# Token halves interleaved in the tail of a fused attention and feed-forward kernel

## The chip, the cores and the metric

The kernel runs on one core of a Trainium2 chip. The metric is the device time of one execution in microseconds (us). The core's engines work from queues of their own and meet only at semaphores: TensorE (PE in the profile), VectorE (DVE), ScalarE (ACT), GpSimd (POOL) and SyncE (SP), which issues all the transfers.

## The reference

The input is x of shape (4, 256, 256), that is 1024 tokens of width 256, and a context of (4, 256, 64). Four blocks follow one another, each with a residual. What matters for the change:

```
x = x + L0_xattn(layernorm(x), ctx, ...)      # 16 heads
x = x + L0_ffn(layernorm(x), w_fc, w_proj)    # both products on values rounded to fp8:
    h = square(relu(fp8(x) @ fp8(w_fc).T));  out = fp8(h) @ fp8(w_proj).T
    # one scale over the whole of h: no token of h can be rounded before all are there
x = x + L1_xattn(ctx, ctx, mask, qc_score=layernorm(x)):
    softmax(mask(((q @ Wq.T + bq) @ (k @ Wk.T + bk).T / 8) * layernorm(x)))
x = x + L1_ffn(layernorm(x)):
    h  = x + (rmsnorm(x) @ wv + bv) @ wo
    h2 = rmsnorm(h)
    y  = h + (silu(h2 @ w_gate) * (h2 @ w_up)) @ w_down    # 704 inner columns
    x where the router's score of the token is not over 0.5
```

After h has been rounded, everything is row by row: token t needs only its own row.

## The kernel before, in words

The 1024 tokens are 8 tiles of 128 (NT = 8). The program is one queue of instructions for each engine, written out by hand; there is no scheduler, and an instruction waits behind every earlier one of its engine. The first attention block fills the first 260 us. The change is in what comes after.

**GpSimd after the attention loop.** It makes the attention mask `mbias` (four steps of two instructions, L460 and L461, one step for each batch), scales the weights `wg` by the second norm's weights (L467), and then raises the variances to the power -1/2 (`power(3)`, L391). On this VectorE's `newton(3)` and the input scale of the feed-forward block wait; GpSimd then makes `xn` from `xs` tile by tile (L475), which ScalarE and VectorE turn into fp8 values `x8`. After that it scales `wu`, and serves eight more powers, in the order of their number. TensorE's `expand` (L1298) makes h from `x8`; VectorE's relu (L871) and ScalarE's square follow.

**Rounding of h.** When the largest of h is known (L890), ScalarE writes two scaled copies of each token tile (L633, L635) and VectorE makes of them the rounded tile `h8` in two instructions over 1024 elements (L978 and L981). TensorE contracts the tile with `wpr8` (L1352, into bank 4 + t % 4), and VectorE adds the product to `xs` and takes its statistics (`x2_tile`, L896 and L899). VectorE's order before is tile by tile: h8(t), then x2_tile(t-2). All eight h8 come first, then the scores of the first half.

**The halves.** From there on the tokens go in two halves of 4 tiles each, `gr` 0 and 1, each through this chain on VectorE, with GpSimd's power and ScalarE between:
- `gate_scores` (L908), `newton`, `mask_scores` (L916), `largest` (L922); ScalarE's exponentials `softmax` (L640)
- `x3_tiles` (L928 to L934) and statistics; `norm_tiles` (newton, L698, L944 to L946)
- TensorE turns `xn` (`turn_norm`, L1055), ScalarE copies it (`turned_copy`, L498), TensorE multiplies with `wvo` (`attend`, L1365)
- `h_tiles` (newton, L955, L957), ScalarE's squares (L651), `h_square` (L962), `h2_tiles` (newton, L971)
- TensorE turns `h2`, ScalarE copies it to `tailT`, and the gate stage begins.

**Gate stage.** 12 steps n = 0 to 11, six for each half: 8 matmuls of 512 columns (L1389), Silu on ScalarE (L662), the product on VectorE (L1016). Step n needs the product of step n-2. The second half's chain hangs between these steps: in all three queues there are lines `if n == 1`, `if n == 2` and so on that say after which step a piece of it comes. VectorE also computes the router's scores (L1027) at n = 4 and adds the base rows (L1036), which GpSimd has summed in one long instruction (L489). Then 8 contractions with `wd` (L1407), each followed by two VectorE instructions and a transfer out.

**Fillers.** `keep_busy(n, spare)` (L1273) issues n matmuls of 512 columns, whose results nobody reads, in TensorE's queue. Before, 6 of them stand ahead of each contraction, 50 after the last x2 and 18 ahead of the turning of h2.

Of the kernel before, what the change touches and what calls it, by code (L numbers as in the profile page):

```python
# [12 lines left out]
ALU = mybir.AluOpType  # L13
# [9 lines left out]
P = 128  # L23
B, S, D = 4, 256, 256
TOK = B * S
NT = TOK // P
# [79 lines left out]
def build(nc, x, ctx_t, ctx_n, blob, const_a, const_b, wq1_t, wk1_t, attn_mask, key_mask,  # L106
          w_fc_t, w_proj_t, small, w_router, wv_t, wo, w_gate, w_up, w_down, out):
    with ExitStack() as ctx:
# [126 lines left out]
        ident16_ready = sem("ident16_ready")  # L235
        norm_ready = sem("norm_ready")
        turned = sem("turned")
# [143 lines left out]
        def _(pool):  # L381
# [67 lines left out]
            for k in range(DK):  # L449
# [6 lines left out]
                                        ALU.mult))  # L456
            for b in range(B):
                mb = mbias[:, 2 * b:2 * b + 2, :]
                kb = ktmp[:, b * S:(b + 1) * S].unsqueeze(1).to_broadcast([P, 2, S])
                in_order(pool.tensor_scalar(mb, mA[:], MASKED, None, ALU.mult))  # L460
                ins = pool.tensor_tensor(mb, mb, kb, ALU.add)  # L461
            ins.then_inc(mbias_ready, 1)


# [4 lines left out]

            pool.wait_ge(d_ffn1, 64)  # L470
            scale_rows(wg)
            power(3, c_ve[:], minus_half[:], c_y[:])
            pool.wait_ge(inv_ready, 1)
            for t in range(NT):
                pool.tensor_scalar(xn[:, t, :], xs[:, t, :], negmean[:, t:t + 1], xscale[:, t:t + 1],  # L475
                                   ALU.add, ALU.mult).then_inc(v_ready, 1)
            scale_rows(wu)

# [4 lines left out]

            for n, gr in ((4, 0), (5, 1), (6, 0), (7, 0), (8, 0), (9, 1), (10, 1), (11, 1)):
                powers(n, gr)

            pool.wait_ge(norm_ready, 3 * NT)
            pool.wait_ge(h2_ready, NT)
# [4 lines left out]
        def _(act):  # L493
# [163 lines left out]
            for n in range(2 * FT1):  # L657
                m = min(P, FF1 - n % FT1 * P)
                act.wait_ge(gate_ready, n + 1)
                if n >= 2:  # L660
                    act.wait_ge(act_ready, n - 1)
                act.activation(silu(n)[0:m, :], bank[2 * (n % 2)][0:m, :], ACT.Silu).then_inc(silu_ready, 1)  # L662
                if n == 1:
                    turned_copy(8, tailT, turned_copied, (2, 3))
                if n == 2:
                    h_squares(1)
                if n == 4:
                    turned_copy(10, tailT, turned_copied, (2, 3))
# [3 lines left out]
        def _(dve):  # L672
# [220 lines left out]
            def x2_tile(t):  # L893

                dve.wait_ge(mlp_ready, t + 1)
                dve.scalar_tensor_tensor(out=xs[:, t, :], in0=bank[4 + t % 4][:, 0:D], scalar=sc[:, 2:3],  # L896
                                         in1=xs[:, t, :], op0=ALU.mult, op1=ALU.add).then_inc(x2_ready, 1)
                dve.wait_ge(x2_ready, t + 1)
                return dve.bn_stats(stats[:, t, :], xs[:, t, :])  # L899
# [5 lines left out]
            def gate_scores(gr):  # L905

                for t in range(*groups[gr]):
                    dve.scalar_tensor_tensor(out=xn[:, t, :], in0=xs[:, t, :], scalar=mv[:, t, 0:1], in1=qk1[:, t, :],  # L908
                                             op0=ALU.subtract, op1=ALU.mult).then_inc(norm_ready, 1)

            def mask_scores(gr):
                lo, hi = groups[gr]
                newton(4 + gr, rstd, lo, hi)
                dve.wait_ge(norm_ready, NT + hi)
# [9 lines left out]
            def x3_tiles(gr):  # L924
# [10 lines left out]
                in_order(ins)  # L935
                aggregate(6 + 3 * gr, lo, hi)

            def norm_tiles(gr):

                lo, hi = groups[gr]  # L940
                newton(6 + 3 * gr, rstd, lo, hi)
                for t in range(lo, hi):
                    normalise(t).then_inc(norm_ready, 1)
                in_order(dve.tensor_tensor(c_ve[:, lo:hi], rstd[:, lo:hi], rstd[:, lo:hi], ALU.mult))  # L944
                in_order(dve.tensor_tensor(c_ve[:, lo:hi], c_ve[:, lo:hi], mv[:, lo:hi, 1], ALU.mult))
                dve.tensor_scalar(c_ve[:, lo:hi], c_ve[:, lo:hi], 1e-6, None, ALU.add).then_inc(variance_ready, 1)  # L946

            def h_tiles(gr):

                newton(7 + 3 * gr, r1, *groups[gr])  # L950
                dve.wait_ge(vo_copied, 3)
                dve.wait_ge(norm_ready, 2 * NT + groups[gr][1])
                for t in range(*groups[gr]):
# [11 lines left out]
            def h2_tiles(gr):  # L965

                lo, hi = groups[gr]
                dve.wait_ge(variance_ready, 8 + 3 * gr)
                newton(8 + 3 * gr, r2, lo, hi)
                for t in range(lo, hi):  # L970
# [3 lines left out]

            for t in range(NT + 2):
                if t < NT:
                    dve.wait_ge(square_ready, t + 1)
                    dve.scalar_tensor_tensor(out=hv[t % 3], in0=hm[t % 3], scalar=1.5 * 2.0 ** 14, in1=hv[t % 3],  # L978
                                             op0=ALU.max, op1=ALU.subtract).then_inc(step_ready, 1)
                    dve.wait_ge(step_ready, t + 1)  # L980
                    dve.scalar_tensor_tensor(out=h8[:, :, t * P:(t + 1) * P],  # L981
                                             in0=hm[t % 3].rearrange("p (f s) -> p f s", f=FT0), scalar=1.5 * 2.0 ** 14,
                                             in1=hv[t % 3].rearrange("p (f s) -> p f s", f=FT0),
                                             op0=ALU.max, op1=ALU.subtract).then_inc(h8_ready, 1)
                if t == NT:

                    dve.wait_ge(mbias_ready, 1)
                    dve.wait_ge(qk_copied, 8)
                    gate_scores(0)
                    mask_scores(0)  # L990
                    largest(0)
                if t >= 2:
                    ins = x2_tile(t - 2)
                if t == half + 1:
                    in_order(ins)
                    aggregate(4, 0, half)
            in_order(ins)
            aggregate(5, half, NT)
# [12 lines left out]

            for n in range(2 * FT1):
# [34 lines left out]
        def _(pe):  # L1047
# [296 lines left out]
            keep_busy(10, 3)  # L1344
            for t in range(NT):
                if t:
                    keep_busy(6, 3)
                pe.wait_ge(h8_ready, t + 1)
                if t >= 4:
                    pe.wait_ge(x2_ready, t - 3)  # L1350
                for ft in range(FT0):
                    ins = pe.matmul(bank[4 + t % 4][:, 0:D], h8[:, ft, t * P:(t + 1) * P], wpr8[:, ft, :],  # L1352
                                    start=(ft == 0), stop=(ft == FT0 - 1))
                ins.then_inc(mlp_ready, 1)


            def turn_norm(c):
                turn(1, lambda t: xn[:, t, :], norm_ready, 2 * NT, (2 * c, 2 * c + 1))

# [20 lines left out]
            for n in range(2 * FT1):  # L1380
# [111 lines left out]
```

## Time and profile before

| | us |
|---|---|
| median of 3 runs | 459.43 (459.09 to 460.18) |
| the profiled execution's own time | 459.85 |
| its span | 458.1 |
| busy: PE / DVE / ACT / POOL | 410.2 / 304.5 / 202.8 / 178.5 |
| chain that ended last, by engine | PE 61%, DVE 20%, ACT 7%, POOL 5% |

The span is what the engines' records cover; the time of the execution is 1.75 us longer. The busy share of PE counts the fillers. In the page's 40 slices (11.45 us each) TensorE is busy 9 tenths or more up to 275 us, with few exceptions; the slices from 275 us on have the digits 5, 6, 9, 6, 8, 6, 3, 9, 8, and 9 after that. The granted clock (PEclk, 9 is full) has 5, 9, 8, 8, 9, 6, 8, 9, 7 in the slices from 286 us on, and 9 after that.

### The profile page before, as it was taken

Reading aid. Unit: us, or ns where it says so; the run is one execution under the profiler, and the core shown is the slowest. Engines: PE = TensorE matmul, PEld = TensorE weight load, DVE = VectorE, ACT = ScalarE, POOL = GpSimd, SP = SyncE. Lnnn points to the kernel's source line nnn. Section 1 sums busy time; section 2 is a strip of 40 time slices with the busy share of each in tenths; the row PEclk is TensorE's granted clock in tenths of the full one; section 3 lists DMA queues with packets and bytes.
Section 4 is the critical chain, followed back from the end, with each engine's and each line's share of the span. In section 5 each row is a group of like instructions: output and inputs, shape, how many; then the busy total and the mean of one; then the engine's idle time right before and its main releaser. Section 6 shows DMA issues by size and latency. Waiting matters only on the chain.

```text
span 458.1 us, 5998 instructions
## 1 busy us (share of the span) xinstructions
PE 410.2 (90%) x2029; PEld 247.9 (54%) x2029; DVE 304.5 (66%) x681; ACT 202.8 (44%) x551; POOL 178.5 (39%) x164
## 2 busy tenths in 40 slices
PE   1898999999999999999999995696863989999997
PEld 1765666666566666665667872342431444634475
DVE  5778679677686766767775653586999576483322
ACT  1525466464565555555578523267931024321100
POOL 2554554655546455464631189630010101040000
PEclk9999999999999999999999999598896897999999
DMA  8643020110201000021000140000000000000011
GB/s 263 213 154 123 2 92 1 49 46 0 93 0 71 24 1 1 0 73 55 1 1 1 26 140 0 0 1 1 0 1 0 0 2 0 0 0 1 1 46 46
DMA packets 9085, 17.51 MB, mean 38 GB/s; under 512 B 2144, under 2 KB 6944, under 8 KB 8160
## 3 DMA queue, kind: packets, MB, share of 16 engines
q1 hardware_dynamic: 9056, 17.14, 11.1%
q8 instruction: 16, 0.26, 0.2%
q14 instruction: 13, 0.11, 0.1%
HBM read 16.09 MB, written 1.05 MB: 37 GB/s over the span
## 4 chain that ended last, share of the span: by engine, by line
PE 61%; DVE 20%; ACT 7%; POOL 5%; issue 4%; DMA 2%; SPq 0%; DVEq 0%; ACTq 0%
PE bank L1389 8%; PE bank L1153 5%; PE bank L1407 5%; PE bank L1178 5%; PE bank L1060 5%; PE bank L1166 4%; PE bank L1062 4%; PE bank L1061 4%; PE bank L1184 4%; DVE rot_up L737 3%; PE bank L1138 3%; PE bank L1273 3%; PE bank L1083 3%; ACT prob L557 3%; DVE tail_all L981 2%
## 5 line engine op out<-in xcount | busy, mean ns | idle before, releaser
L410 POOL TENSOR_TENSOR prob<-prob,rinv 128x512 f32<-128x512 f32 x64 | 66.6, 1042 | 106.4 <-DVE rinv L795 106.4
L557 ACT ACTIVATE prob<-bank,negmax 128x256 f32<-128x256 f32 x128 | 60.1, 480 | 40.6 <-DVE negmax L790 40.6
L790 DVE TENSOR_REDUCE negmax<-bank 128x2 f32<-128x512 f32 x64 | 41.2, 687 | 25.1 <-PE bank L1153 24.6
L391 POOL TENSOR_TENSOR c_y<-c_ve,minus_half 128x4 f32<-128x4 f32 (+1 forms) x11 | 12.8, 1166 | 98.2 <-DVE c_ve L694 69.3
L1389 PE MATMUL bank<-tailT,blobs 128*128 128x512 f32 (+1 forms) x96 | 45.6, 630 | 1.5 <-ACT tailT L498 0.8
L548 ACT COPY probT<-bank 128x512 f32<-128x512 f32 x64 | 37.8, 591 | 19.6 <-PE bank L1166 19.4
L1273 PE MATMUL bank<-wfc,ident 128*128 128x512 bf16 x144 | 40.4, 434 | 6.6 <-DVE xs L896 6.2
L405 POOL TENSOR_TENSOR rot_low<-rot_low,rot_up 128x512 f32<-128x512 f32 x32 | 40.9, 1277 | 12.0 <-DVE rot_up L737 12.0
L737 DVE TENSOR_TENSOR rot_up<-bank,cb 64x512 f32<-64x512 f32 x64 | 44.1, 689 | 0.9
L1060 PE MATMUL bank<-xnT,w 128*128 128x512 f32 x96 | 42.0, 437 | 1.5 <-DVE xnT L713 1.0
L1166 PEld LDWEIGHTS bank<-ca,prob 128*128 128x128 f32 x256 | 30.5, 141 | 18.9 <-issue 16.2
L1166 PE MATMUL bank<-ca,prob 128*128 128x128 f32 x256 | 38.9, 275 | 1.8 <-ACT probT L548 1.1
L735 DVE TENSOR_TENSOR rot_low<-bank,cb 128x512 f32<-128x512 f32 x32 | 22.1, 689 | 26.4 <-PE bank L1062 26.4
L1062 PE MATMUL bank<-xnT,w 128*128 128x512 f32 x96 | 37.9, 395 | 0.0
L1061 PE MATMUL bank<-xnT,w 128*128 128x512 f32 x96 | 37.6, 392 | 0.0
L1178 PE MATMUL bank<-probT,kva 128*64 128x256 f32 x256 | 34.7, 392 | 2.2 <-ACT probT L548 1.4
L1153 PE MATMUL bank<-ktmp,uT 64*128 64x256 f32 x256 | 36.3, 402 | 0.0
L569 ACT COPY cT<-bank 128x256 f32<-128x256 f32 x32 | 11.9, 373 | 46.7 <-PE bank L1178 46.7
L1389 PEld LDWEIGHTS bank<-tailT,blobs 128*128 128x128 f32 (+1 forms) x96 | 18.0, 193 | 26.5 <-issue 24.7
L1184 PE MATMUL bank<-wkvo,cT 128*128 128x256 f32 x128 | 30.9, 384 | 0.5 <-ACT cT L569 0.5
L1153 PEld LDWEIGHTS bank<-ktmp,uT 64*128 64x128 f32 x256 | 22.0, 186 | 13.7 <-issue 12.3
L1273 PEld LDWEIGHTS bank<-wfc,ident 128*128 128x128 bf16 x144 | 15.2, 109 | 24.9 <-issue 8.7
(186 smaller groups left out, 706.7 us busy)
## 6 DMA issues: line engine op xcount, KB each, us to landing
blobs<-in_blob SPq DMA_DIRECT2D x7, 1024.0 KB, 4.8
xs<-in_x SPq DMA_DIRECT2D x2, 512.0 KB, 4.0
xn<-in_w_fc_t SPq DMA_DIRECT2D x1, 1024.0 KB, 4.9
ctxT<-in_w_proj_t SPq DMA_DIRECT2D x1, 1024.0 KB, 5.3
out<-qk SPq DMA_DIRECT2D x8, 128.0 KB, 1.7
cb<-in_const_b SPq DMA_DIRECT2D x1, 768.0 KB, 8.4
blobs<-in_w_gate SPq DMA_DIRECT2D x1, 704.0 KB, 4.2
blobs<-in_w_up SPq DMA_DIRECT2D x1, 704.0 KB, 7.0
```

What stands on the lines that cost most here:

```text
L410: pool.tensor_tensor(p[:], p[:], rinv[:, n % PROBS, :].unsqueeze(2).to_broadcast([P, 2, S]), ALU.mult).then_inc(normed, 1)
L557: ins = act.activation(prob[n % PROBS][:, st, :], pS[n % 2][:, st * S:(st + 1) * S], ACT.Exp, bias=negmax[:, n % 2, st:st + 1], accum_out= ...
L737: ins = dve.tensor_tensor(tokens(crossed[to:to + DC, :]), tokens(src[lo:lo + DC, :]), angles(sinq, r, lo, lo + DC), ALU.mult)
L1060: pe.matmul(o, a[0], b[0], start=start, stop=False)
L1061: pe.matmul(o, a[0], b[1], start=False, stop=False)
L1062: return pe.matmul(o, a[1], b[0], start=False, stop=stop)
L1153: ins = pe.matmul(pS[h][:, st * S:(st + 1) * S], uT[b // 2][lo:hi, at:at + P], ktmp[lo:hi, b * S:(b + 1) * S], start=True, stop=True)
L1166: ins = pe.transpose(pT[:, lt * S + st * P:lt * S + (st + 1) * P], prob[n % PROBS][:, st, lt * P:(lt + 1) * P], ident)
L1178: ins = pe.matmul(pV[b % 2][h * DC:(h + 1) * DC, 0:S], kva[:, 2 * b + lt, :], probT[h][:, lt, :], start=(lt == 0), stop=(lt == 1))
L1184: return pe.matmul(bank[OUT_BANK[t // 2]][:, t % 2 * D:(t % 2 + 1) * D], cT[:, f, t * P:(t + 1) * P], wkvo[:, f, :], start=(f == 0 and t % ...
L1273: pe.matmul(bank[spare][:], ident16[:], wfc8[:, 0, 0:CH], start=True, stop=True)
L1389: ins = pe.matmul(bk[0:m, :], w[:, k, ft * P:ft * P + m], tailT[:, k, c * CH:(c + 1) * CH], start=(k == 0), stop=(k == DK - 1))
```

## The change

The computation is the same. In GpSimd's queue two of the four mask steps and both scalings of weights come after the making of `xn`; the powers are asked for in another order (the first half's four, then the second half's). VectorE's order is written out: the first half's scores come after h8(4) and its own four x2 tiles, and the second half's h8 and x2 tiles stand between the steps of the first half's chain. TensorE's contractions are spread accordingly, with other numbers of fillers, into banks 6 and 7 in place of four banks, which adds a wait for an older x2 tile. In the gate stage the second half's pieces hang on later steps, the router's scores come at n = 6, and the base rows are added two at a time from n = 8.

```diff
 # GpSimd
-            for b in range(B):
+            def mask_rows(b):
...
-            pool.wait_ge(d_ffn1, 64)
-            scale_rows(wg)
+            for b in range(2):
+                mask_rows(b)
             power(3, c_ve[:], minus_half[:], c_y[:])
             pool.wait_ge(inv_ready, 1)
             for t in range(NT):
                 pool.tensor_scalar(xn[:, t, :], ...).then_inc(v_ready, 1)
+            for b in range(2, B):
+                ins = mask_rows(b)
+            ins.then_inc(mbias_ready, 1)
+            pool.wait_ge(d_ffn1, 64)
+            scale_rows(wg)
             scale_rows(wu)
-            for n, gr in ((4, 0), (5, 1), (6, 0), (7, 0), (8, 0), (9, 1), (10, 1), (11, 1)):
+            for n, gr in ((4, 0), (5, 0), (6, 0), (7, 0), (8, 1), (9, 1), (10, 1), (11, 1)):
                 powers(n, gr)
 # ScalarE, in the gate stage
-                if n == 1:
+                if n == 3:
                     turned_copy(8, tailT, turned_copied, (2, 3))
-                if n == 2:
+                if n == 4:
                     h_squares(1)
-                if n == 4:
+                if n == 5:
                     turned_copy(10, tailT, turned_copied, (2, 3))
 # VectorE (x2_tile reads bank[6 + t % 2] in place of bank[4 + t % 4])
-            for t in range(NT + 2):
...
-            x3_tiles(0)
-            gate_scores(1)
-            norm_tiles(0)
-            h_tiles(0)
-            h_square(0)
-            mask_scores(1)
-            h2_tiles(0)
-            largest(1)
-            x3_tiles(1)
-            norm_tiles(1)
+            for t in range(3):
+                h8_tile(t)
+            x2_tile(0)
+            h8_tile(3)
+            x2_tile(1)
+            h8_tile(4)
+            x2_tile(2)
+            in_order(x2_tile(3))
+            aggregate(4, 0, half)
+            dve.wait_ge(mbias_ready, 1)
+            dve.wait_ge(qk_copied, 8)
+            gate_scores(0)
+            mask_scores(0)
+            largest(0)
+            h8_tile(5)
+            x2_tile(4)
+            x3_tiles(0)
+            h8_tile(6)
+            x2_tile(5)
+            norm_tiles(0)
+            h8_tile(7)
+            x2_tile(6)
+            h_tiles(0)
+            h_square(0)
+            in_order(x2_tile(7))
+            aggregate(8, half, NT)
+            h2_tiles(0)
+            gate_scores(1)
+            mask_scores(1)
+            largest(1)
 # VectorE, in the gate stage
-                if n == 2:
+                if n == 0:
+                    x3_tiles(1)
+                if n == 1:
+                    norm_tiles(1)
+                if n == 4:
                     h_tiles(1)
-                if n == 3:
                     h_square(1)
                     h2_tiles(1)
-                if n == 4:
+                if n == 6:
... # the router's scores
-                t = n - 4
-                if 0 <= t:
+                if n >= 8:
                     dve.wait_ge(base_ready, 1)
-                    dve.tensor_tensor(atbuf(t), atbuf(t), qk1[:, t, :], ALU.add).then_inc(base_added, 1)
+                    for t in (2 * n - 16, 2 * n - 15):
+                        dve.tensor_tensor(atbuf(t), atbuf(t), qk1[:, t, :], ALU.add).then_inc(base_added, 1)
 # TensorE
-            for t in range(NT):
-                if t:
-                    keep_busy(6, 3)
+            def contract(t):
                 pe.wait_ge(h8_ready, t + 1)
-                if t >= 4:
-                    pe.wait_ge(x2_ready, t - 3)
+                if t >= 2:
+                    pe.wait_ge(x2_ready, t - 1)
...
-            pe.wait_ge(x2_ready, NT)
-            keep_busy(50, 3)
+            contract(0)
+            for t in range(1, 5):
+                keep_busy(6, 3)
+                contract(t)
+            keep_busy(32, 3)
+            contract(5)
+            keep_busy(16, 3)
+            contract(6)
+            keep_busy(4, 3)
             turn_norm(0)
             attend(0)
-
+            contract(7)
             pe.wait_ge(wgu_ready, 2)
-            keep_busy(18, 7)
+            keep_busy(14, 4)
             turn(2, hbuf, h2_ready, 0, (0, 1))
...
-                if n == 1:
+                if n == 3:
+                    pe.wait_ge(x2_ready, NT)
                     turn_norm(1)
-                if n == 2:
+                if n == 4:
                     attend(1)
-                if n == 4:
+                if n == 5:
                     turn(2, hbuf, h2_ready, 0, (2, 3))
```

Left out are the new numbers of the semaphore counts, which follow the new order, and a semaphore `gate_done` that counts the products of L908, which `norm_ready` counted before.

## Rows read from the trace of the kernel before

**Rows 1.** Chain that ended last, 255 to 300 us: start us, length us, what.
```profile
282.10 4.05 POOL blobs L467 x2
286.16 1.64 POOL c_y L391
290.81 1.93 PE bank L1318 x4
```
**Rows 2.** Timeline, 255 to 296 us: start us, length us, engine and line [idle before].
```profile
279.78 0.17 DVE L694 TENSOR_SCALAR c_ve<-mv 128x8 f32<-128x8 f32 x1
287.89 0.17 DVE L684 TENSOR_TENSOR c_t<-c_y 128x8 f32<-128x8 f32 x1 [7.39 <-POOL c_y L391]
```
**Rows 3.** Timeline of VectorE, rounding of h to the first half's scores.
```profile
297.95 0.88 DVE L865 SCALAR_TENSOR_TENSOR tail_all<-bf_m,xn 128x256 bf16<-128x256 bf16 x1
...
334.33 0.48 DVE L896 SCALAR_TENSOR_TENSOR xs<-bank,sc,xs 128x256 f32<-128x256 f32 x1
...
337.57 0.48 DVE L896 SCALAR_TENSOR_TENSOR xs<-bank,sc,xs 128x256 f32<-128x256 f32 x1
...
345.67 1.66 DVE L908 SCALAR_TENSOR_TENSOR xn<-xs,mv,qk 128x256 f32<-128x256 f32 x4
...
349.73 1.22 DVE L922 TENSOR_REDUCE c_m<-xn 128x4 f32<-128x1024 f32 x1
```
**Rows 4.** Timeline of VectorE, the first half's chain after its exponentials.
```profile
353.30 0.18 DVE L928 RECIPROCAL c_r<-ssq 128x4 f32<-128x4 f32 x1
...
356.96 0.17 DVE L694 TENSOR_SCALAR c_ve<-mv 128x4 f32<-128x4 f32 x1
...
359.57 1.38 DVE L698 TENSOR_SCALAR xn<-xs,mv,rstd 128x256 f32<-128x256 f32 x4
...
361.25 0.17 DVE L946 TENSOR_SCALAR c_ve<-c_ve 128x4 f32<-128x4 f32 x1
...
368.75 0.48 DVE L955 SCALAR_TENSOR_TENSOR cT<-bank,r,cb 128x256 f32<-128x256 f32 x1 [5.44 <-PE bank L1365]
...
372.83 0.17 DVE L962 TENSOR_SCALAR c_ve<-ssq 128x4 f32<-128x4 f32 x1 [0.57 <-ACT mbias L651]
...
375.43 0.16 DVE L684 TENSOR_TENSOR c_t<-c_y 128x4 f32<-128x4 f32 x1
...
376.22 1.14 DVE L971 TENSOR_SCALAR cT<-cT,r 128x256 f32<-128x256 f32 x4
```
**Rows 5.** Timeline of TensorE, 290 to 460 us.
```profile
352.25 13.63 PE L1273 MATMUL bank<-wfc,ident 128*128 128x512 bf16 x50 [6.25 <-DVE xs L896]
...
367.48 3.72 PE L1365 MATMUL bank<-cb,tailT 128*128 128x256 f32 x16 [0.73 <-ACT tailT L498]
...
379.00 10.08 PE L1389 MATMUL bank<-tailT,blobs 128*128 128x512 f32 x16 [0.82 <-ACT tailT L498]
...
405.58 7.28 PE L1389 MATMUL bank<-tailT,blobs 128*64 128x512 f32 x16
413.58 17.58 PE L1389 MATMUL bank<-tailT,blobs 128*128 128x512 f32 x40 [0.72 <-DVE cT L1016]
431.08 1.99 PE L1407 MATMUL bank<-wd,tail_all 128*128 128x256 f32 x8
```
**Rows 6.** Timeline of ScalarE, between the second exponentials and the first Silu.
```profile
380.84 1.28 ACT L662 ACT_TABLE_LOAD   x1
```
**Rows 7.** Busy time by stretch: PE, PEld, DVE, ACT, POOL; PEclk is the granted clock.
```profile
375.00:379.00 4.00, 1.63 (x9) 0.97 (x9) 3.32 (x10) 1.22 (x3) 0.00 (x0) 0.89 0.01 2
379.00:382.00 3.00, 3.00 (x4) 1.45 (x5) 1.11 (x4) 2.98 (x9) 0.00 (x0) 0.50 0.00 0
```
**Rows 8.** Timeline of VectorE at the router's first score.
```profile
405.35 4.43 DVE L1027 SCALAR_TENSOR_TENSOR ctxT<-xn,wr 128x256 f32<-128x256 f32 x1
```
**Rows 9.** Timeline of GpSimd, 270 to 460 us.
```profile
339.22 2.07 POOL L391 TENSOR_TENSOR c_y<-c_ve,minus_half 128x4 f32<-128x4 f32 x1 [37.35 <-DVE c_ve L694]
...
404.98 4.51 POOL L489 TENSOR_TENSOR qk<-xs,xn 128x2048 f32<-128x2048 f32 x1 [2.18 <-DVE cT L971]
```

More of the change, by code:

```diff
@@ L235, in build @@
         ident16_ready = sem("ident16_ready")
-        norm_ready = sem("norm_ready")
+        norm_ready, gate_done = sem("norm_ready"), sem("gate_done")
         turned = sem("turned")
@@ L460, in _ @@
                 in_order(pool.tensor_scalar(mb, mA[:], MASKED, None, ALU.mult))
-                ins = pool.tensor_tensor(mb, mb, kb, ALU.add)
-            ins.then_inc(mbias_ready, 1)
+                return pool.tensor_tensor(mb, mb, kb, ALU.add)
             def scale_rows(w):
@@ L482, in powers @@
                 power(n, c_ve[:, lo:hi], minus_half[:, lo:hi], c_y[:, lo:hi])
-            for n, gr in ((4, 0), (5, 1), (6, 0), (7, 0), (8, 0), (9, 1), (10, 1), (11, 1)):
+            for n, gr in ((4, 0), (5, 0), (6, 0), (7, 0), (8, 1), (9, 1), (10, 1), (11, 1)):
                 powers(n, gr)
-            pool.wait_ge(norm_ready, 3 * NT)
+            pool.wait_ge(norm_ready, 2 * NT)
             pool.wait_ge(h2_ready, NT)
@@ L895, in x2_tile @@
                 dve.wait_ge(mlp_ready, t + 1)
-                dve.scalar_tensor_tensor(out=xs[:, t, :], in0=bank[4 + t % 4][:, 0:D], scalar=sc[:, 2:3],
+                dve.scalar_tensor_tensor(out=xs[:, t, :], in0=bank[6 + t % 2][:, 0:D], scalar=sc[:, 2:3],
                                          in1=xs[:, t, :], op0=ALU.mult, op1=ALU.add).then_inc(x2_ready, 1)
@@ L908, in gate_scores @@
                     dve.scalar_tensor_tensor(out=xn[:, t, :], in0=xs[:, t, :], scalar=mv[:, t, 0:1], in1=qk1[:, t, :],
-                                             op0=ALU.subtract, op1=ALU.mult).then_inc(norm_ready, 1)
+                                             op0=ALU.subtract, op1=ALU.mult).then_inc(gate_done, 1)
             def mask_scores(gr):
                 lo, hi = groups[gr]
-                newton(4 + gr, rstd, lo, hi)
-                dve.wait_ge(norm_ready, NT + hi)
+                newton(4 + 4 * gr, rstd, lo, hi)
+                dve.wait_ge(gate_done, hi)
                 for t in range(lo, hi):
@@ L935, in x3_tiles @@
                 in_order(ins)
-                aggregate(6 + 3 * gr, lo, hi)
+                aggregate(5 + 4 * gr, lo, hi)
             def norm_tiles(gr):
                 lo, hi = groups[gr]
-                newton(6 + 3 * gr, rstd, lo, hi)
+                newton(5 + 4 * gr, rstd, lo, hi)
                 for t in range(lo, hi):
@@ L948, in h_tiles @@
             def h_tiles(gr):
-                newton(7 + 3 * gr, r1, *groups[gr])
+                newton(6 + 4 * gr, r1, *groups[gr])
                 dve.wait_ge(vo_copied, 3)
-                dve.wait_ge(norm_ready, 2 * NT + groups[gr][1])
+                dve.wait_ge(norm_ready, NT + groups[gr][1])
                 for t in range(*groups[gr]):
@@ L967, in h2_tiles @@
                 lo, hi = groups[gr]
-                dve.wait_ge(variance_ready, 8 + 3 * gr)
-                newton(8 + 3 * gr, r2, lo, hi)
+                dve.wait_ge(variance_ready, 7 + 4 * gr)
+                newton(7 + 4 * gr, r2, lo, hi)
                 for t in range(lo, hi):
                     dve.tensor_scalar(hbuf(t), hbuf(t), r2[:, t:t + 1], None, ALU.mult).then_inc(h2_ready, 1)
-            for t in range(NT + 2):
[L976 to L996, printed above, removed]
@@ L997, in _, with h8_tile @@
-            in_order(ins)
-            aggregate(5, half, NT)
+            def h8_tile(t):
+                dve.wait_ge(square_ready, t + 1)
+                dve.scalar_tensor_tensor(out=hv[t % 3], in0=hm[t % 3], scalar=1.5 * 2.0 ** 14, in1=hv[t % 3],
+                                         op0=ALU.max, op1=ALU.subtract).then_inc(step_ready, 1)
+                dve.wait_ge(step_ready, t + 1)
+                dve.scalar_tensor_tensor(out=h8[:, :, t * P:(t + 1) * P],
+                                         in0=hm[t % 3].rearrange("p (f s) -> p f s", f=FT0), scalar=1.5 * 2.0 ** 14,
+                                         in1=hv[t % 3].rearrange("p (f s) -> p f s", f=FT0),
+                                         op0=ALU.max, op1=ALU.subtract).then_inc(h8_ready, 1)
@@ L1344, in _ @@
             keep_busy(10, 3)
-            for t in range(NT):
-                if t:
-                    keep_busy(6, 3)
+            def contract(t):
                 pe.wait_ge(h8_ready, t + 1)
-                if t >= 4:
-                    pe.wait_ge(x2_ready, t - 3)
+                if t >= 2:
+                    pe.wait_ge(x2_ready, t - 1)
                 for ft in range(FT0):
-                    ins = pe.matmul(bank[4 + t % 4][:, 0:D], h8[:, ft, t * P:(t + 1) * P], wpr8[:, ft, :],
+                    ins = pe.matmul(bank[6 + t % 2][:, 0:D], h8[:, ft, t * P:(t + 1) * P], wpr8[:, ft, :],
                                     start=(ft == 0), stop=(ft == FT0 - 1))
@@ L1357, in turn_norm @@
             def turn_norm(c):
-                turn(1, lambda t: xn[:, t, :], norm_ready, 2 * NT, (2 * c, 2 * c + 1))
+                turn(1, lambda t: xn[:, t, :], norm_ready, NT, (2 * c, 2 * c + 1))
             def attend(c):
```

## Prediction

> **What bounds the kernel now.** I read the page's slices first. TensorE is busy nearly everywhere up to 275 us, and not in the slices behind it: whatever the change gains, it gains there. Then the chain that ended last, for who sets the time in those slices, and then each engine's timeline, for durations. Two places stand out.
>
> First, after the attention loop the chain runs through GpSimd. The variances are written at 279.78 + 0.17 = 279.95 [rows 2], but GpSimd is still at mask steps and at scaling `wg` (until 286.15), and only then raises them to the power, 1.64 us [rows 1]. VectorE sits idle 7.39 us ahead of 287.89 [rows 2]. The next steps (maximum over partitions, input scale, `xn`) hang on that one value.
>
> Second, from 320 to 352 us VectorE is the bound: it rounds a tile of h and adds a tile of x2 every 337.57 - 334.33 = 3.24 us [rows 3], while ScalarE and GpSimd have nothing to do and TensorE mostly runs fillers. Then it turns round: 50 fillers start at 352.25, when the last x2 is there, and take 13.63 us [rows 5]; `xn` of the first half is ready at 359.57 + 1.38 = 360.95 [rows 4], and TensorE reaches it only at about 365.9. VectorE idles 5.44 us ahead of 368.75 [rows 4]. From 379.00 on TensorE is nearly solid: 52.08 us to the start of the down projections at 431.08 [rows 5], and those last to the end.
>
> **The change part by part.** I work on the clock of the trace of before, in which VectorE reaches x2_tile(2) at 334.33, and take GpSimd's part off at the end.
>
> *GpSimd's order.* Two mask steps (as before) end ahead of 279.95, so power(3) starts about there and not at 286.16 [rows 1]: 6.1 us earlier, and VectorE's newton with it, since its other operands were there when the 7.39 us of idle time began. What is late next? TensorE's four matmuls of L1318 took 1.93 us [rows 1] after a long idle stretch; with the pause 6 us shorter I expect full clock there, half the time, and ScalarE, which waited for them, gains up to 0.7 us against GpSimd's tiles. Against it stands what GpSimd now does beside the rounding of x8: two mask steps and two scalings that are no longer behind it or ahead. VectorE's L863 and L865 read two tensors in SBUF. Beside GpSimd's two-input instruction such an instruction waited until that ended: 4.43 us in place of some 0.4 beside L489 [rows 8, 9]. Beside GpSimd's one-input scaling two of eight were lengthened, to 0.88 as in [rows 3]. So the two L461 instructions can each hold VectorE up for their length, of which I count about 0.7 in all. Bounds: 0 and 2.5. The two small terms cancel: 6.1 us. The rest of GpSimd's work ends some 9 us later than its old place and lies beside relu (which reads PSUM and SBUF once) and before the first user of `mbias`; it hides. Its wait for the weights' transfers costs nothing, as they landed before 282; SyncE's queue isn't touched.
>
> The Trainium skill (SBUF — State Buffer, Who interferes with whom) says that a VectorE instruction with two SBUF inputs and a GpSimd instruction that reads SBUF exclude each other for the whole of the one that came first. The row of L1027 agrees; the eight instructions beside the scaling, most of them at their usual length, do not bear it out in full.
>
> *First half's scores earlier.* x2_tile(2) starts at 334.33 as before. h8(5) no longer stands between: x2_tile(3) ends at 336.05, statistics and aggregate to 336.75, the scores block runs 345.67 to 350.95 = 5.28 [rows 3], so `largest` ends at 342.0; if the power runs as long as its longest (2.07 against 1.0 [rows 9]) 0.5 later. I take 342.15. Exponentials take the 2.1 us to 344.25, behind h8(5) on VectorE (3.24 - 0.86 = 2.38 [rows 3]), which ends at 344.5. The x2 of tile 4 to 345.35. x3_tiles: 353.30 to 357.13 = 3.83 [rows 4], to 349.25. h8(6) and x2(5) 3.24, to 352.5; they cover the power, even at 2.07. norm_tiles: newton 0.79 (375.43 to 376.22), then 359.57 to 361.42 = 1.85 [rows 4], to 355.1. h8(7) and x2(6) to 358.35, newton to 359.15.
>
> TensorE meanwhile: xn's fourth tile at 354.6, turning and copies some 1.5 (for h2 it was 377.36 to 379.00 = 1.64 [rows 4, 5]), so attend starts at 356.05 and takes 3.72 [rows 5] to 359.8. h_tiles is bound by VectorE: 368.75 to 372.26 is 3.5 [rows 4], so 359.15 to 362.6; h_square 0.57 later [rows 4], 363.45. The power of 1.0 and newton of 0.8 cover x2(7) and the aggregate (1.5). h2 starts at 365.8, against 376.22 [rows 4]: 10.4 us earlier. The new waits of contract(t) for x2(t-2) cost 0.4 us or less in TensorE's queue, where nothing but fillers is behind. The fillers: 32 take 7.2 us at full clock (50 took 13.63 with the first 5 us at half clock [rows 5]) against the 8.6 us until h8(5); 16 take 3.6 against 6.1. So contractions come on time, with pauses of 1.4 and 2.5 us. Those can bring the clock down ahead of attend(0): at half clock all through, attend ends at 363.5, h_tiles 2.0 us later than said. Range 0 to 2.0; nearest is 0, as VectorE has 1.9 us of slack on attend's last tile.
>
> *Gate stage.* It starts 10.4 us earlier, at 368.6 for 379.00 [rows 5]. VectorE does the second half's scores after h2 (367.0 + 5.3 = 372.3), exponentials to 374.4, table load 1.28 [rows 6], first Silu ready 376.4, product 377.1. The first matmul group took 6.6 us of the 10.08 [rows 5] at half clock [rows 7], so to 375.2: no stall from the new order. x3_tiles(1) 3.83 delays the second product to 381.6; step 3 needs it at 382.1. norm_tiles(1) ends 384.8, turning 386.4, attend(1) is after step 4: 389.8 to 393.3. Silu and product of step 4, newton, h_tiles, squares, power, newton: h2 of the second half at 398.1. Step 5 (3.4 us) ends on TensorE at 396.8: 1.4 us of stall. Turning and copies 2.8 (376.22 to 379.00 [rows 4, 5]), which no matmul step covers now: step 6 starts at 400.8. Before it started at 409.2 (half of the 7.28 us from 405.58 [rows 5]). So of 10.4 us 2.0 are given back: 8.4. The 0.72 us ahead of 413.58 [rows 5] goes, since the product of step 5 no longer waits behind a router score that GpSimd's L489 holds up [rows 8, 9]; the scores now come at step 6 (some 2.9 us), when L489 (from 399.2 on, 4.51) is done. 9.1. Steps 7 to 11 and the down projections are TensorE-bound as before; two base additions per step (0.7 us) fit in 3.4.
>
> *The clock.* From 396.8 to 400.8 TensorE has a pause, thin transposes and a pause. That is the pattern of 375 to 379 us, 1.63 us busy of 4.00, after which the clock was 0.50 [rows 7] for some 6.4 us, which cost 3.2. The other such place before, around 404 us, had no drop, but its pause was only 0.4. Ends 0 and 3.2; the rows allow either, the likeness is to the first, the phase is open. I take half, 1.6.
>
> Sum: 6.1 + 9.1 - 1.6 = 13.6. On the profiled execution (459.85, span 458.1) that is 446.2; it stands 0.4 above the median, so on the median 459.43 I say 445.8.
>
> **The rivals.**
>
> *A, the exclusive lock holds for every pair.* Then each of the seven or so roundings of x8 left when the masks resume waits for a whole GpSimd instruction: 2 x 1.5, 2 x 1.3, 3 x 2.0 (L467 is 4.05 for two [rows 1]) = 11.6 in place of 3.0, 8.6 lost: 454.4. For: the 4.43 [rows 8]. Against: only two of eight lengthened beside the scaling. It is what the page cited above would give.
>
> *B, GpSimd's head start is lost* because another input of the scale chain is late (TensorE's vo products or a table on ScalarE): 3 us of 6.1 remain, 448.9. Against: VectorE's 7.39 idle us name only the power.
>
> *C, the clock never recovers between 336 and 384* (slower). Fillers are counts, so at half clock 32 take 13.7 us and 16 take 6.8: contract(6) at 359, turning at 363, attend to 373, contract(7) and 14 fillers to 381, step 0 at 384 instead of 379.00. With the longer gate stage (53.4 for 52.1 us) and its drop of 3.2 the down projections start 9.5 us later, less 6.1: 3.4 slower, 462.8. It decides from the point at which the 32 fillers outlast h8(5) by more than 7 us. Against it: in the page's slice at 332 us TensorE is busy 6 tenths, with the same 3.24 us cycle, and its clock has the full digit.
>
> *D, the second half's chain is longer than worked out*: every us by which h2(1) is late is a us of TensorE's stall. If two of its hand-offs cost 1.5 us more each, and the clock drops fully: 450.5.
>
> **How the numbers follow.** Forecast with its clock cases 0.70 (442.5 to 449.0), A 0.08, B 0.07, D 0.10, C 0.03, and 0.02 that the parts cancel to nothing. 442 to 451 leaves out A, C and the rest, with something for misses on the fast side: about 2 in 10. A change within 0.2% is what a measurement can't tell from none. Faster 0.95, same 0.01, slower 0.04.
>
> **What would show it.** GpSimd's eight-column power starts within 0.3 us of the variances. The first half's exponentials come some 15 us earlier than before (8.8 here and 6.1 by GpSimd). 32 fillers end before h8(5). Step 0 of the gates 16.5 us earlier than 379.00, step 6 about 14.5 earlier than 409.2 with TensorE idle ahead of it. The clock after step 6's start says which end of the 3.2 us it is. Wrong would be: VectorE's L863 and L865 near 1.3 us each, contractions waiting on fillers, or a stall ahead of step 3.

## The result, and the profile after

The changed kernel takes 445.38 us in the median of four runs (443.75 to 446.39), against 459.26 (458.03 to 460.18): a ratio of 0.970, 95% interval 0.9676 to 0.9724, or 13.9 us less. The prediction was 445.8. The profiled execution is the fastest of the four, 443.75 with a span of 442.0, so its trace shows 16.1 us of span, not 13.9. Here and below, executions over 1.5% slower than the fastest of the same kernel are left out of the ratios, not out of the medians.

The trace of after, along the path. First GpSimd and VectorE around the power of the variances (timeline; start, length, engine, line, what ended the idle time before):

```profile
279.06 0.17 DVE L697 TENSOR_SCALAR c_ve<-mv 128x8 f32<-128x8 f32 x1
279.31 1.67 POOL L391 TENSOR_TENSOR c_y<-c_ve,minus_half 128x8 f32<-128x8 f32 x1 [3.55 <-DVE c_ve L697]
281.08 0.17 DVE L687 TENSOR_TENSOR c_t<-c_y 128x8 f32<-128x8 f32 x1 [1.27 <-POOL c_y L391]
285.45 0.44 DVE L866 SCALAR_TENSOR_TENSOR xn<-bf_m,xn 128x256 f32<-128x256 bf16 x1 [1.15 <-ACT bf_m L588]
291.27 0.82 DVE L866 SCALAR_TENSOR_TENSOR xn<-bf_m,xn 128x256 f32<-128x256 bf16 x1
292.92 1.41 DVE L868 SCALAR_TENSOR_TENSOR tail_all<-bf_m,xn 128x256 bf16<-128x256 bf16 x1
295.14 0.69 DVE L874 TENSOR_SCALAR_CACHE_REDUCE cT<-bank 128x512 f32<-128x512 f32 x1 [0.81 <-PE bank L1309]
```

GpSimd now waits for the variances (3.55 us), not they for it, and the 7.39 us of VectorE's idle time in [rows 2] are 1.27. The two long roundings (0.82 and 1.41 us) are the price beside the mask steps.

VectorE in the interleaved stretch:

```profile
326.84 0.48 DVE L899 SCALAR_TENSOR_TENSOR xs<-bank,sc,xs 128x256 f32<-128x256 f32 x1
333.36 1.22 DVE L925 TENSOR_REDUCE c_m<-xn 128x4 f32<-128x1024 f32 x1
337.74 0.16 DVE L931 RECIPROCAL c_r<-ssq 128x4 f32<-128x4 f32 x1
351.41 0.48 DVE L958 SCALAR_TENSOR_TENSOR cT<-bank,r,cb 128x256 f32<-128x256 f32 x1
357.96 1.14 DVE L974 TENSOR_SCALAR cT<-cT,r 128x256 f32<-128x256 f32 x4
368.36 0.69 DVE L1024 TENSOR_TENSOR tail_all<-bank,tail_all 128x512 f32<-128x512 f32 x1 [4.05 <-ACT tail_all L665]
```

L958 has no idle time before it any more (5.44 in [rows 4]): from 326.84 to 357.96 VectorE is the bound, with its longest wait 0.57 us, ahead of L965.

TensorE, fillers (L1284) and gate stage (L1404):

```profile
328.33 7.07 PE L1284 MATMUL bank<-wfc,ident 128*128 128x512 bf16 x32
344.12 1.68 PE L1361 MATMUL bank<-wpr,tail_all 128*128 128x256 bf16 x8 [2.59 <-DVE tail_all L984]
360.74 7.10 PE L1404 MATMUL bank<-tailT,blobs 128*128 128x512 f32 x16 [0.82 <-ACT tailT L501]
369.11 3.70 PE L1404 MATMUL bank<-tailT,blobs 128*128 128x512 f32 x8 [1.26 <-DVE tail_all L1024]
373.56 3.70 PE L1404 MATMUL bank<-tailT,blobs 128*128 128x512 f32 x8 [0.75 <-DVE tail_all L1024]
390.27 1.55 PE L1066 MATMUL bank<-ca,cT 128*128 128x128 f32 x8 [1.68 <-DVE cT L974]
392.56 22.49 PE L1404 MATMUL bank<-tailT,blobs 128*128 128x512 f32 x48 [0.73 <-ACT tailT L501]
414.98 1.99 PE L1423 MATMUL bank<-wd,tail_all 128*128 128x256 f32 x8
```

Busy time by stretch, with the granted clock as the third number from the end of the line:

```profile
345.00:347.00 2.00, 2.00 (x8) 0.99 (x7) 1.88 (x8) 0.00 (x0) 0.00 (x0) 0.50 0.00 0
359.00:362.00 3.00, 2.18 (x9) 1.23 (x10) 2.86 (x11) 1.07 (x2) 0.00 (x0) 1.00 0.03 5
391.00:394.00 3.00, 2.27 (x8) 1.36 (x8) 0.60 (x2) 1.07 (x2) 2.85 (x1) 0.69 0.00 0
394.00:398.00 4.00, 4.00 (x8) 1.62 (x7) 0.00 (x0) 0.22 (x1) 1.66 (x1) 0.80 0.00 0
```

The clock falls to 0.50 behind TensorE's wait of 2.59 us ahead of contraction 6 (first line), but it is full again for `attend` (L1373), which takes 3.72 us as before. It stays full where gate step 0 starts, which before had 0.50 [rows 7]. It is below full in the last two stretches, at the start of step 6, and steps 6 to 11 take 22.49 us.

| milestone | before | after | gained so far | by this part | forecast |
|---|---|---|---|---|---|
| variances written | 279.78 | 279.06 | 0.72 | 0.72 | none |
| newton | 287.89 | 281.08 | 6.81 | 6.09 | 6.1 |
| first rounding of x8 | 293.49 | 285.45 | 8.04 | 1.23 | 0.7 |
| relu starts | 302.55 | 295.14 | 7.41 | -0.63 | -0.7 |
| x2 of tile 2 | 334.33 | 326.84 | 7.49 | 0.08 | 0 |
| gate step 0 | 379.00 | 360.74 | 18.26 | 10.77 | 10.4 |
| gate step 6 | 409.2 | 392.56 | 16.6 | -1.6 | -2.0 |
| down projections | 431.08 | 414.98 | 16.10 | -0.5 | -0.9 |

### The profile page after: what moved, and what is told of

Read it like the earlier page. It is cut to its first block, busy times and chain, and to the rows that moved or that the text cites. A ratio compares the mean times of both kernels' runs of the same rounds, so it can differ in the third digit from the quotient of the medians.

```text
span 442.0 us, 5954 instructions
## 1 busy us (share of the span) xinstructions
PE 399.9 (90%) x2003; PEld 244.4 (55%) x2009; DVE 301.1 (68%) x681; ACT 203.0 (46%) x551; POOL 180.5 (41%) x164
## 4 chain that ended last, share of the span: by engine, by line
PE 62%; DVE 23%; ACT 8%; issue 4%; DMA 1%; POOL 1%; SPq 0%; DVEq 0%; ACTq 0%
PE bank L1404 7%; PE bank L1195 7%; PE bank L1189 6%; PE bank L1164 6%; PE bank L1423 5%; PE bank L1071 5%; PE bank L1177 5%; PE bank L1073 4%; PE bank L1072 4%; DVE rot_up L740 3%; PE bank L1149 3%; PE bank L1094 3%; ACT prob L560 3%; DVE tail_all L984 2%; ACT probT L551 2%
## 5 line engine op out<-in xcount | busy, mean ns | idle before, releaser
L391 POOL TENSOR_TENSOR c_y<-c_ve,minus_half 128x4 f32<-128x4 f32 (+1 forms) x11 | 14.2, 1286 | 83.4 <-DVE c_ve L697 60.2
L1404 PE MATMUL bank<-tailT,blobs 128*128 128x512 f32 (+1 forms) x96 | 44.2, 614 | 3.6 <-DVE tail_all L1024 2.0
L1177 PEld LDWEIGHTS bank<-ca,prob 128*128 128x128 f32 x256 | 30.5, 141 | 18.8 <-issue 16.1
L1404 PEld LDWEIGHTS bank<-tailT,blobs 128*128 128x128 f32 (+1 forms) x96 | 17.5, 188 | 27.8 <-issue 23.2
L1284 PE MATMUL bank<-wfc,ident 128*128 128x512 bf16 x119 | 30.6, 401 | 0.6 <-DVE sc L893 0.3
L560 ACT ACTIVATION_READ_ACCUMULATOR prob<-bank,negmax 128x1 f32 x128 | 26.5, 207 | 0.0
```

What stands on the lines that cost most here:

```text
L560: ins = act.activation(prob[n % PROBS][:, st, :], pS[n % 2][:, st * S:(st + 1) * S], ACT.Exp, bias=negmax[:, n % 2, st:st + 1], accum_out= ...
L1177: ins = pe.transpose(pT[:, lt * S + st * P:lt * S + (st + 1) * P], prob[n % PROBS][:, st, lt * P:(lt + 1) * P], ident)
L1404: ins = pe.matmul(bk[0:m, :], w[:, k, ft * P:ft * P + m], tailT[:, k, c * CH:(c + 1) * CH], start=(k == 0), stop=(k == DK - 1))
```

## The experiments

The medians below stand beside runs of the kernel before on the same chip: 459.14 for the first four, 459.10 for the next four, 458.81 for the last four. The changed kernel's 445.38 stands beside 459.26, so the ratios are the stricter comparison with it.

**GpSimd's order alone**, on the kernel before.

```diff
... # the loop over all four mask steps goes; L467's scaling of wg goes from here
+            for b in range(2):
+                mask_rows(b)
             power(3, c_ve[:], minus_half[:], c_y[:])
... # xn, then
+            for b in range(2, B):
+                ins = mask_rows(b)
... # the semaphore of the mask, the wait for the weights
+            scale_rows(wg)
             scale_rows(wu)
```

> The kernel before with GpSimd's new order alone (two mask steps and both scalings of weights after xn). Theory: the power of the variances starts 6.1 us earlier and everything behind it moves with it, plus about 1.2 us because TensorE is still at full clock for the matmuls of the bias fold: 452.0 us (7.3 faster than before). Rival B (something else in the scale chain is late next): only about 3 us faster, 456.

Measured: 452.34 us, ratio 0.985 (0.983 to 0.987), 6.8 less. Rival B, under which this run was expected at 456, is out.

**GpSimd's order undone**, on the changed kernel: the same lines the other way.

> The changed kernel with GpSimd's order of before. Theory: the two halves of the change add up, so this loses about 7 us of the 13.9 and takes 452.4. If the interleaving needs the head start of GpSimd, it loses more (455 or above); if GpSimd's part was hidden in the changed kernel, it stays near 446.

Measured: 452.43 us, ratio 0.985 (0.982 to 0.988). So the order on GpSimd is worth 7 us with and without the interleaving, and the interleaving is worth 6.7 to 6.9 with and without the order: two changes that add up.

**28 fillers for 50**, on the kernel before.

```diff
-            keep_busy(50, 3)
+            keep_busy(28, 3)
```

> The kernel before with 28 fillers in place of 50 ahead of the turning of xn, nothing else. If the 4.9 us by which the fillers outlasted xn were simply lost, this gains 4 to 5 us (about 454.7), and the interleaving proper is worth only the rest of its 8 to 9 us. Rival: with fewer fillers the clock is low in the attention product and the gate stage and the gain is under 1.5 us (458 or more).

Measured: 454.11 us, ratio 0.989 (0.986 to 0.991), 5.0 less. TensorE's timeline of that kernel; the transposes (L1055) come right behind the fillers:

```profile
352.68 7.47 PE L1273 MATMUL bank<-wfc,ident 128*128 128x512 bf16 x27 [6.65 <-DVE xs L896]
360.07 1.73 PE L1055 MATMUL bank<-ca,xn 128*128 128x128 f32 x8
374.37 9.69 PE L1389 MATMUL bank<-tailT,blobs 128*128 128x512 f32 x16 [0.77 <-ACT tailT L498]
```

So one number on the kernel before brings 5.0 us, where the interleaving, fillers and all, brings 6.9. What the reordering brings beyond that, 1.9 us, is small because it gives back in the gate stage a part of what it gains ahead of it. Two traces with the same order on GpSimd show it, this one and that of gpsimd_undone: counted from the variances, the interleaved kernel starts gate step 0 5.9 us earlier (88.4 for 94.3 us), and from there to the down projections it takes 55.7 us for 51.7, the clock's drop at step 6 included.

**Late mask steps after x8**, on the changed kernel.

```diff
+            pool.wait_ge(x8_ready, NT)
             for b in range(2, B):
                 ins = mask_rows(b)
```

> The changed kernel with GpSimd's two late mask steps waiting until all of x8 is rounded. Theory (GpSimd's two-input instruction holds up VectorE's two-input rounding): the rounding instructions of 0.82 and 1.41 us fall to 0.42 and about 0.5, and the time falls by about 1.0 to 1.4 us against the changed kernel (444.2). Rival: the lengthening comes from elsewhere or is hidden, no difference (445.4).

Measured: 444.17 us, ratio 0.967 (0.964 to 0.970), 1.2 less than the first four runs of the changed kernel, though the two intervals overlap. The trace shows where. VectorE's last two roundings and the start of relu:

```profile
293.50 0.42 DVE L867 SCALAR_TENSOR_TENSOR xn<-bf_m,xn 128x256 f32<-128x256 bf16 x1
293.95 0.42 DVE L869 SCALAR_TENSOR_TENSOR tail_all<-bf_m,xn 128x256 bf16<-128x256 bf16 x1
295.19 0.69 DVE L875 TENSOR_SCALAR_CACHE_REDUCE cT<-bank 128x512 f32<-128x512 f32 x1 [0.81 <-PE bank L1310]
```

From its first rounding (286.89) to relu 8.30 us, against 285.45 to 295.14 = 9.69 in the changed kernel: 1.39 us lost beside the mask steps.

**Gate stage as before**, on the changed kernel.

```diff
+            x3_tiles(1)
+            norm_tiles(1)
... # ahead of step 0; then as before: turning of xn at n == 1, attend and h_tiles at 2,
... # h_square and h2_tiles at 3, turning of h2 and the router at 4
```

> The changed kernel with the second half's pieces, the router and the base rows in the gate stage where they were before (x3 and norm of the second half ahead of step 0, then after steps 1 to 4). Theory: step 2 now waits some 5.5 us for the first product, which stands behind the second half's norm; the exposed turning before step 6 goes (about 3.5 us back) and the router stalls behind GpSimd's long addition again (1 to 2 us lost): about 3 us slower than the changed kernel, 448.4. Rival: the places of the pieces don't matter, since TensorE's work is the same: 445.4.

Measured: 446.31 us, ratio 0.973 (0.971 to 0.974); about 1 us slower than the changed kernel in the medians, with intervals that overlap, and not 3. TensorE:

```profile
361.89 9.44 PE L1403 MATMUL bank<-tailT,blobs 128*128 128x512 f32 x16 [0.77 <-ACT tailT L501]
373.46 2.21 PE L1065 MATMUL bank<-ca,xn 128*128 128x128 f32 x8 [2.13 <-DVE xn L701]
390.52 1.55 PE L1065 MATMUL bank<-ca,cT 128*128 128x128 f32 x8 [0.40 <-DVE cT L974]
399.98 17.58 PE L1403 MATMUL bank<-tailT,blobs 128*128 128x512 f32 x40 [0.71 <-DVE cT L1026]
```

The wait ahead of step 2 is only 2.13 us, as steps 0 and 1 took 9.44 us, partly at half clock, in place of 7.10 and lay over the rest. TensorE waits 0.40 us ahead of the last turning, for 1.68 in the changed kernel. The later places win one thing and lose another.

**Fillers ahead of the last turning**, on the changed kernel.

```diff
                 if n == 5:
+                    pe.wait_ge(act_ready, 5)
+                    keep_busy(7, 0)
                     turn(2, hbuf, h2_ready, 0, (2, 3))
```

> The changed kernel with 7 fillers in TensorE's pause of 1.68 us after gate step 5, ahead of the last turning. Theory (the drop of the clock at steps 6 and 7 costs 1.7 us in the profiled execution and comes from this pause): the granted clock stays at 1.00 behind it and the median falls by 1 to 1.7 us, to 444.0. Rival: the clock isn't set by this pause, or the fillers delay the turning: no gain, 445.4 or up to 0.5 more.

Inconclusive in time: four executions from 443.25 to 452.12, ratio 0.970 (0.962 to 0.979). In the trace of the fastest the clock is full; its stretch behind the turning, and TensorE's steps 6 to 11:

```profile
394.00:398.00 4.00, 4.00 (x11) 1.77 (x10) 0.09 (x1) 0.60 (x1) 2.65 (x1) 1.00 0.00 0
```
```profile
393.54 21.01 PE L1404 MATMUL bank<-tailT,blobs 128*128 128x512 f32 x48 [0.73 <-ACT tailT L501]
```

These are 1.48 us less than 22.49. One trace doesn't show that the clock's drop came from the pause, but the traces together make it likely. In the four kernels that fill the pause (this one, and the three below that do real work in it) steps 6 to 11 take 21.01 us in each trace. With the pause of 1.67 or 1.68 us left in place they take 22.49, 22.62 (changed_again), 23.50 (masks_after_x8) and 23.98 us (gpsimd_undone), and in one trace, product_first, 21.01 as well. So with the pause the drop can come, and costs from nothing to 3.0 us.

**Real work in the pause**, on the changed kernel.

```diff
                 if n == 5:
+                    pe.wait_ge(act_ready, 4)
+                    pe.wait_ge(h_ready, 5)
+                    for f in range(3):
+                        down_part(0, f)
                     turn(2, hbuf, h2_ready, 0, (2, 3))
+                    down_part(0, 3)
... # the first down projection then does only ft 4 and 5
```

> The changed kernel with real work in the same pauses: 3 of the 6 accumulation steps of the first down projection ahead of the last turning, a fourth behind it (about 0.5 us each). Theory: TensorE is the bound from step 6 to the end, so the 2.0 us moved out of the end are gained, and the clock is held up as with fillers (another 1 to 1.7): 442.4. Rival: only the moved work counts, 443.4; if the pause isn't on the path, 445.4.

Measured: 441.77 us, ratio 0.962 (0.960 to 0.964), 3.6 less than the changed kernel, with intervals apart. TensorE, with the parts at L1397; steps 6 to 11 run at full clock:

```profile
391.65 1.56 PE L1397 MATMUL bank<-wd,tail_all 128*128 128x256 f32 x6
393.39 1.55 PE L1066 MATMUL bank<-ca,cT 128*128 128x128 f32 x8 [0.18 <-DVE cT L974]
394.77 0.60 PE L1397 MATMUL bank<-wd,tail_all 128*128 128x256 f32 x2
395.66 21.01 PE L1409 MATMUL bank<-tailT,blobs 128*128 128x512 f32 x48 [0.29 <-ACT tailT L501]
```

**Products first in the gate stage**, on the changed kernel.

```diff
-                if n == 0:
+                if n == 1:
                     x3_tiles(1)
-                if n == 1:
+                if n == 2:
                     norm_tiles(1)
```

> The changed kernel with the second half's x3 tiles after the product of gate step 1 and its norm after that of step 2 (one step later each). Theory: TensorE's stalls ahead of steps 2 and 3 (1.26 and 0.75 us on VectorE) become about 0.3, while the chain of the second half starts 0.6 us later and its turning stalls some 0.5: about 0.8 us faster, 444.6. Rival: the second half's chain, not the products, sets step 6, and the time is the same or 0.6 longer (445.4 to 446.0).

443.95 us, ratio 0.969 (0.963 to 0.974): in the direction expected, but not told apart from the changed kernel, and the trace speaks for the rival. The four steps 0 to 3 run without a gap, but the stall moves to the turning, which it makes 0.69 us late, and the turning holds up step 4:

```profile
362.21 15.55 PE L1404 MATMUL bank<-tailT,blobs 128*128 128x512 f32 x32 [0.82 <-ACT tailT L501]
378.46 1.65 PE L1066 MATMUL bank<-ca,xn 128*128 128x128 f32 x8 [0.69 <-DVE xn L701]
394.53 21.01 PE L1404 MATMUL bank<-tailT,blobs 128*128 128x512 f32 x48 [0.73 <-ACT tailT L501]
```

From step 0 to step 6 it is 32.3 us, against 31.8 in the trace of after: half a us lost. This execution gains it back only by the clock, which happened to stay full behind the pause ahead of step 6.

**The last three together** (mask steps, real work in the pause, products first), and the same with 26 fillers for 16 ahead of contraction 6.

> The changed kernel with the late mask steps after x8, the partial down projection in the pauses, and the products first in the gate stage, all three. Theory: they lie at three places of the path and add up, 1.2 + 3.6 + 1.0 = 5.8 us less than the changed kernel, 439.6. Rival: the stall moves from one to the next (a product earlier only lengthens the pause before step 6), and together they give no more than the best of them, 441.8.

> As the combined kernel, with 26 fillers in place of 16 ahead of contraction 6, which close the pause of 2.6 us there. Theory (single executions of 448 to 452 us, with a mean clock of 0.965, come from the clock falling in this pause): the median is the same and the highest execution stays within 2 us of it. Rival: the slow executions have another source and still come, or 26 fillers delay contraction 6 and the time rises by 1 us.

Measured: 440.49 us, ratio 0.959 (0.955 to 0.963), and 441.86 us, ratio 0.964 (0.961 to 0.967). The first is the fastest version here, 4.8 us under the changed kernel on the same chip (445.27) with intervals apart; from the work in the pause alone (0.960 to 0.964) it isn't told apart. Its six executions go from 438.21 to 445.34, so that the expected 439.6 is reached in some executions and not in others. The products first are the doubtful part: in the traces of these two kernels steps 0 to 6 take 33.5 and 33.7 us, in that of the work in the pause alone 31.8. The late mask steps and the work in the pause without the third were not run. The 26 fillers close the pause (0.43 us for 2.60) and change nothing for the better; executions of 444.35 and 445.26 still come, so they don't come from that pause alone.

**No late fillers**: the changed kernel without its last 66.

```diff
-            keep_busy(32, 3)
... # and 16, 4 and 14 further down
```

> The changed kernel without its 66 fillers from the one before contraction 5 on (32, 16, 4 and 14). They cost nothing where they stand in VectorE's shadow, so their worth is only the clock: theory, half clock in attend (up to 2.0 us on the path) and in the first 3 to 6 us of the gate stage (1.5 to 3 us): 449. Rival C's inverse: the fillers themselves are late work and the time doesn't change or falls, 445 or less.

The theory missed, and the rival holds: 444.62 us, ratio 0.968 (0.966 to 0.970). The clock does fall: its mean is 0.956 to 0.965 in the five executions near 444.6, where the changed kernel has 0.979 to 0.988 in five of its six on the same chip. Nothing on the path minds. The trace is of the sixth execution, 452.66 us; its stretches and TensorE's `attend` (L1373):

```profile
338.00:341.00 3.00, 0.00 (x0) 0.00 (x0) 2.83 (x10) 0.00 (x0) 0.00 (x0) 0.50 0.00 0
350.00:354.00 4.00, 2.47 (x10) 1.40 (x10) 3.79 (x12) 0.00 (x0) 1.00 (x1) 0.50 0.00 0
```
```profile
356.04 3.72 PE L1373 MATMUL bank<-cb,tailT 128*128 128x256 f32 x16 [0.68 <-ACT tailT L501]
368.58 16.01 PE L1400 MATMUL bank<-tailT,blobs 128*128 128x512 f32 x32 [0.77 <-ACT tailT L501]
```

Contractions at half clock lie under VectorE's work, `attend` finds the clock full again (3.72 us), and the slower start of the gate stage lies under the exponentials and the table load that the first product waits for. From contraction 4, behind which the first fillers are left out, to gate step 6 it is 65.1 us in this trace, and 65.1 in the trace of after.

**The changed kernel again.**

> The changed kernel itself, on the same chip as the three others, so that they are compared with it directly. Expected 445.4, with executions between 443.5 and 446.5; if slow executions belong to the change, one in five or so near 450.

445.27 us, ratio 0.970 (0.967 to 0.973), as in the first runs; one of six executions took 452.23, and no trace shows that one.

## Why the prediction was right, point by point

*GpSimd's order: right.* 6.09 us for 6.1 in the trace, 6.8 alone in time. The two small terms that I let cancel were 1.23 and -0.63 (forecast 0.7 and -0.7): the bias fold's four matmuls (L1329) took 1.11 us at full clock, as expected, and with them the two small steps of the maximum ahead of them. The price of the shared access is 1.39 us by the experiment, inside 0 to 2.5 and twice what I took; the table's -0.63 is against the kernel before, which had long roundings of its own beside the scaling [rows 3].

*Rival A, the full lock: wrong in its size, right for one kind.* Beside the two-input L461 a rounding of 0.42 us took 1.41, and ended 0.29 us after L461 did. Beside the one-input L460 one rounding took 0.82 us, and two others, in the same 1.65 us, their usual 0.42. Beside the one-input making of `xn` (L473) L866 took its usual 0.41 and L868 mostly 0.58, once 0.67. The Trainium skill (SBUF — State Buffer, Who interferes with whom) makes no such difference: by it each GpSimd instruction here, as all of them read SBUF, holds up a rounding that comes after it to its end. The trace agrees for L461 and not for the one-input ones.

*First half's chain: right*, 10.77 for 10.4, step by step. All the hand-offs that I had to cover were covered. `attend` took 3.72 us, the favourable end of the 0 to 2.0 us left open for it. But the prediction doesn't say how much of the 10.4 one number would bring: it named the fillers' 4.9 us as a place where time is lost and didn't separate it. fillers_28 does: 5.0.

*Gate stage: the sum right, one term wrong.* I took half clock for step 0 (6.6 us); the clock was 1.00. The 3.2 us this should have freed didn't show, because the first product waits for exponentials and table load anyway: TensorE stalled 1.26 and 0.75 us ahead of steps 2 and 3, and steps 0 to 6 took 31.8 us for 32.2. The traces of gpsimd_undone and fillers_last_turn confirm it: there steps 0 to 2 took 12.23 and 12.07 us, partly at half clock, and it was 31.8 us from step 0 to step 6 all the same.

*The clock behind the last turning: the mechanism likely right, the size luck.* The pause was 1.68 us for 1.4. The 1.6 us were half of an open range of 0 to 3.2, and the traces with this pause have 0, 1.5, 1.6, 2.5 and 3.0 us. The trace of after happens to lie in the middle.

*Rival C* didn't happen: the 32 fillers took 7.07 us, at full clock, and ended 1.63 us ahead of contraction 5. What it would have cost with the clock down and the fillers in place wasn't tested. Without the late fillers the half clock cost nothing, since VectorE carries this stretch.

*The sum: closer than its parts.* Leaving out the 0.72 us of the start, the parts of the table add up to 15.4 us, 1.8 more than the 13.6 forecast; every part but the first came out a little better. The medians moved by 13.9, since the trace of after is of the fastest execution (mean clock 0.988) and the three others, at 0.976 to 0.979, took 1.6 to 2.6 us longer. That the forecast lies 0.4 us from the median is partly luck.

*Rivals B and D* didn't happen: GpSimd's order alone brought 6.8 us, not about 3, and the second half's chain took no longer than worked out.

## What to carry to other kernels

A queue entry that only has to be done "sometime" must not stand ahead of the one small instruction that everybody waits for; look for the engine named as releaser of a long idle time, and for what it did until then. Count fillers against the arrival they bridge: those that outlast it are lost time (5.0 us here), and those under another engine's bound were worth nothing here. Where work is interleaved, look for later work of the bounding engine to put into the pauses that arise on it; here it brought 3.6 us. And compare more than one trace of a kernel before believing a gain of 1 or 2 us.

## What the runs showed of the hardware that I had not expected

The earlier path has lost a cover. After the attention loop TensorE has short pauses, and in some executions the clock is 0.50 from about 280 us on. With GpSimd's power as late as before, this costs nothing: in the trace of gpsimd_undone TensorE's eight products of `vo` take 3.78 us in place of 1.99, and VectorE still waits 7.38 us for the power alone. With the power early, the products are on the path to the input scale. The combined kernel's profiled execution (444.38 us) has the half clock there, the one with 26 fillers (442.44 us) has not, and up to there the two run the same program. First combined, its products, the step of VectorE that comes behind them, and the clock; then combined_26:

```profile
281.97 3.78 PE L1323 MATMUL bank<-wos,wvs 128*128 128x256 f32 x8
286.00 0.29 DVE L856 TENSOR_REDUCE sc<-bank 128x1 f32<-128x128 f32 x1 [2.86 <-PE bank L1289]
282.00:284.00 2.00, 2.00 (x6) 1.64 (x6) 0.97 (x6) 0.68 (x1) 0.00 (x0) 0.50 0.00 0
```
```profile
281.31 1.99 PE L1323 MATMUL bank<-wos,wvs 128*128 128x256 f32 x8
283.97 0.29 DVE L856 TENSOR_REDUCE sc<-bank 128x1 f32<-128x128 f32 x1 [0.42 <-PE bank L1289]
```

VectorE waits 2.86 us for 0.42. From the variances to relu it is 17.1 us with the half clock (279.95 to 297.08) and 14.7 without (280.36 to 295.05): 2.4 us. The trace of down_in_pause, against that of after, gives the same 2.4 us (18.5 for 16.1). Whether fillers ahead of the `vo` products would keep the clock up there wasn't tried.

The start of the span moves by 1.5 us between executions with the first weights' arrival: TensorE's first matmul started at 8.45 us in one trace and 9.98 in another, and the variances were written 279.06 to 280.54 us in. A comparison of two single traces has this in it (0.72 us of the 16.1 here).
